# Degree sums of a graph network's adjacency build: added by GpSimd, or by transfers that add as they write

## The reference, cut to what matters

```
def _L0_gnn_ref(x, W_lin, W_agg, edge_index):
    row, col = (edge_index[0], edge_index[1])
    msgs = x[row]
    summed = jax.ops.segment_sum(msgs, col, num_segments=num_nodes)
    count = jax.ops.segment_sum(jnp.ones((row.shape[0],), x.dtype), col, num_segments=num_nodes)[:, None]
    agg = summed / jnp.maximum(count, 1.0)
    out = agg @ W_agg.T + x @ W_lin.T
    ...
```

## Time and profile before

| | |
|---|---|
| median of 3 runs | 3345.48 us (3345.35 to 3350.49) |
| span of the profiled execution | 3347.6 us |
| TensorE busy, of the span | 65% |
| VectorE busy | 68% |
| ScalarE busy | 25% |
| GpSimd busy | 49% |
| GpSimd's 48 additions (L633) | 159.9 us in all |
| build, first to last matmul | 360.4 to 848.3 us |

### The profile page before, as it was taken

The page is one execution under the profiler, slowest core; times in us unless marked ns, Lnnn a source line. Parts: engine busy times, 40 slices in busy tenths (PEclk is TensorE's granted clock), DMA queues, the critical chain, the costliest instruction groups (busy, mean ns, idle before and its releaser), DMA issues.

```text
span 3347.6 us, 46752 instructions
## 1 busy us (share of the span) xinstructions
PE 2186.4 (65%) x12603; PEld 1297.7 (39%) x12659; DVE 2262.1 (68%) x3125; ACT 846.9 (25%) x1397; POOL 1645.1 (49%) x1455
## 2 busy tenths in 40 slices
PE   0488877777895989995963444444567665528563
PEld 0233455454453455553443111111366621107563
DVE  8999898898558720055133454444987799979777
ACT  0099433232002020022100111111244322206442
POOL 7400133333047777777104777777876777710000
PEclk9799999999997999997986555565559999965897
DMA  2000010110443523400724433345348733530453
GB/s 71 0 0 0 25 49 39 44 44 39 148 137 84 164 60 96 94 1 1 158 59 94 117 113 112 112 116 104 93 153 268 240 110 110 107 37 0 134 175 94
DMA packets 195115, 301.52 MB, mean 90 GB/s; under 512 B 120540, under 2 KB 133818, under 8 KB 194922
## 3 DMA queue, kind: packets, MB, share of 16 engines
q1 hardware_dynamic: 138986, 175.88, 16.5%
q0 software_dynamic: 40512, 62.87, 10.3%
q10 hardware_dynamic: 15552, 61.94, 6.0%
HBM read 191.65 MB, written 88.01 MB: 84 GB/s over the span
## 4 chain that ended last, share of the span: by engine, by line
PE 35%; POOL 19%; issue 16%; DVE 16%; DMA 6%; ACT 5%; ACTq 1%; DVEq 0%; SPq 0%; POOLq 0%; PEldq 0%
POOL arena L1313 18%; PE PS L538 11%; PE PS L699 9%; PE PS L884 6%; DMA arena<-T_att,idx 5%; ACT arena L514 4%; DVE arena L559 4%; PE PS L981 3%; PE PS L476 2%; DVE arena L1204 1%; PE PS L968 1%; DVE arena L374 1%; DVE arena L490 1%; POOL W L1322 1%; DVE arena L567 1%
## 5 line engine op out<-in xcount | busy, mean ns | idle before, releaser
L1313 POOL DMA_INDIRECT arena<-T_att,idx x864 | 843.7, 976 | 316.9 <-issue 224.8
L538 PE MATMUL PS<-arena 128*128 128x400 f16 (+2 forms) x4320 | 782.5, 332 | 270.0 <-issue 109.7
L538 PEld LDWEIGHTS PS<-arena 128*128 128x128 f16 (+2 forms) x4320 | 529.9, 158 | 512.9 <-issue 349.8
L1148 DVE TENSOR_REDUCE arena<-PS 128x1024 f32 (+1 forms) x432 | 502.2, 1212 | 321.6 <-PE PS L1115 321.6
L1486 POOL DMA_INDIRECT order<-arena x400 | 504.8, 1262 | 246.5 <-issue 246.5
L559 DVE TENSOR_SCALAR arena<-arena 128x1600 f16<-128x1600 f16 x448 | 385.7, 905 | 64.4 <-PE PS L538 60.4
L1115 PE MATMUL PS<-arena,pick 128*128 128x512 bf16 x812 | 315.8, 488 | 157.0 <-DVE arena L1148 143.2
L699 PE MATMUL PS<-arena 128*128 128x512 f16 (+1 forms) x1575 | 317.6, 361 | 88.3 <-issue 75.2
L633 POOL TENSOR_TENSOR rdeg<-rdeg,arena 128x1600 f32<-128x1600 f32 x48 | 159.9, 3331 | 313.4 <-ACT arena L617 313.4
L1104 PE MATMUL PS<-ident_b,score_buf 128*32 128x128 bf16 x864 | 90.0, 268 | 307.1 <-ACT score_buf L1077 297.4
L699 PEld LDWEIGHTS PS<-arena 128*128 128x128 bf16 x1575 | 147.8, 99 | 254.1 <-issue 102.3
(11 more groups left out here) (257 smaller groups left out, 2786.0 us busy)
## 6 DMA issues: line engine op xcount, KB each, us to landing
spill<-arena SPq DMA_DIRECT2D x108, 560.0 KB, 2.8
arena<-spill ACTq DMA_DIRECT2D x108, 560.0 KB, 3.9
arena<-A SPq DMA_DIRECT2D x50, 800.0 KB, 4.5
A<-arena SPq DMA_DIRECT2D x50, 400.0 KB, 2.4
arena<-A SPq DMA_DIRECT2D x50, 400.0 KB, 3.2
arena<-T_att,idx POOLq DMA_INDIRECT x864
order<-arena POOLq DMA_INDIRECT x400
T_att<-h SPq DMA_DIRECT2D x2, 1600.0 KB, 12.3
```

What stands on the lines that cost most here:

```text
L538: return t.matmul(where, lhsT, rhs, start=False, stop=True, skip_group_check=True)
L1148: v.tensor_reduce(cmax[d][:, u:u + 2, bass.ds(i * SLOTS + half * GROUP + q // 2 * QUAD, QUAD)], PS[:, u * BANK:(u + 2) * BANK].rearrange(" ...
L1313: p.indirect_dma_start(out=ring1[:, b, j, :], out_offset=None, in_=T_att[d][:, :], in_offset=bass.IndirectOffsetOnAxis(ap=idx[:, d, k:k + ...
```

## The change

GpSimd no longer adds the strips. It clears `dst_sum` once, and for every cell, when ScalarE has written the strip, it issues a transfer from the strip (f16) to its half of `dst_sum` (f32) that adds to what is there. Two transfers to the same half must not overlap, so GpSimd waits for the one 2 cells before to land. Completion is counted in four semaphores, one for each strip buffer, where one semaphore counted the additions; all waits follow that.

```
-        cell_counted, dst_summed, dst_read = sem("cell_counted"), sem("dst_summed"), sem("dst_read")
+        dst_summed, dst_read = sem("dst_summed"), sem("dst_read")
+        cell_added = [sem(f"cell_added{s}") for s in range(RING_A)]
...
-                    a.wait_ge(cell_counted, c - RING_A + 1)
+                    a.wait_ge(cell_added[c % RING_A], 16 * (c // RING_A))
...
             p.wait_ge(lo_ready, 1)
+            pool_link(p.memset(dst_sum, 0.0))
             for c in range(CELLS):
                 at = dst_sum[:, c % BANDS * BW:(c % BANDS + 1) * BW]
                 p.wait_ge(cell_out, c + 1)
-                if c < BANDS:
-                    p.tensor_copy(at, stage[c % RING_A]).then_inc(cell_counted, 1)
-                else:
-                    p.wait_ge(cell_counted, c - BANDS + 1)
-                    p.tensor_tensor(at, at, stage[c % RING_A], ALU.add).then_inc(cell_counted, 1)
+                if c >= BANDS:
+                    before = c - BANDS
+                    p.wait_ge(cell_added[before % RING_A], 16 * (before // RING_A + 1))
+                p.dma_start(out=at, in_=stage[c % RING_A], accum_op=ALU.add).then_inc(cell_added[c % RING_A], 16)
+
+        def all_added(eng):
+            for s in range(RING_A):
+                eng.wait_ge(cell_added[s], 16 * len(range(s, CELLS, RING_A)))
...
-                t.wait_ge(cell_counted, CELLS)
+                all_added(t)
...
-            v.wait_ge(cell_counted, CELLS)
+            all_added(v)
             place_dve(v, 0)
...
-            a.wait_ge(cell_counted, CELLS)
+            all_added(a)
             ht_act(a, 0)
```

## The result

The changed kernel took 3319.88 us, the median of 4 runs (3318.59 to 3320.83), beside 3347.31 us for the kernel before (3345.35 to 3350.49): a ratio of 0.9918 [0.9904, 0.9932]. It is 27 us faster where 58 were forecast. The profiled spans, 3347.6 and 3319.0 us, differ by 28.6. The time lies in the range that the prediction gave, 3276 to 3336, but more than half of the forecast gain is missing, so a term of the sum was wrong.

A forecast was written before the change was run, and what follows sets the result against it. In the build, GpSimd's additions were taken to hold up VectorE's one-hots, so TensorE ran out of them. -63 + 3 + 2 = -58 us on the profiled 3347.6 made 3289.6, 3287.5 us as median; range 3276 to 3336.

The forecast's parts named there:

- the build: Build of A, 487.9 us long: removing GpSimd's additions was to save 63 us.
- from last strip to first product: End of the build: the last adding transfer was to delay the first strip's load of A by 2 us, ends 0 and 5.
- the prediction's floor and small waits: Build of A: 421.5 us from undisturbed matmul groups and the pauses between them, plus 3 us kept for small waits.
- L: Build: time from one adding transfer's start of issue to the next issue on the same half; 9 us, free below 16.
- the slow rival: Build: GpSimd's wait for landing transfers becomes the new bound, slower from 19.8 us per transfer, 3400 us at 22; chance 12%.
- The rival in which the port is still taken: Build: GpSimd's issues hold VectorE for their length, +22 us, 3310 us; chance 14% together with the clock rival.
- the memset: Before the build: clearing the sums was to hold up VectorE and add 3 us, bounds 0 and 3.3.
- That is the loading of the group's cell numbers (the longer one has the loop's branch besides), and the change leaves it.: Build: TensorE's stands between groups of 8 chunks, 0.89 and 1.31 us alternately, 60.3 us in all, stay as they are.
- so I take the clock at 1.00: Build: TensorE's granted clock rises from 0.94 to 1.00, so 18.9 us of matmul time goes.
- a transfer of over 14 us: Build: one of two signs that the forecast is wrong, one adding transfer taking over 14 us.
- The clock rival: Build: TensorE's clock stays as it is, +19 us, 3306 us; chance 14% together with the rival of the port still taken.
- the idle rival: Build: nothing comes of it, TensorE's stands only move to another wait inside the group, 3345 +- 6 us; chance 4%.

The follow-up runs named there:

- e1_noadd: The changed kernel with no strip added at all, the degree sums left at a constant: 3291.77 us, ratio 0.9836 to the kernel before.
- e12_again: The changed kernel run a second time with no edit: 3318.75 us, ratio 0.991 to the kernel before.
- e8_best: The changed kernel with f16 sums, transfers issued after the next group's first chunk, and plain first transfers instead of the memset: 3290.75 us, ratio 0.9826 to before.
- e11_high: The changed kernel with only the sums of partitions 64 to 127 added, the others constant: 3313.0 us, ratio 0.9897 to the kernel before.
- e10_low: The changed kernel with only the sums of partitions 0 to 63 added, the others constant: 3318.2 us, ratio 0.9913 to the kernel before.

## Why the prediction was right and wrong

**The sum, term by term**, from the two profiles: the build -41.4 us (forecast -63), its start +3.7 (+3), from last strip to first product 15.6 us instead of 13.1, +2.5 (+2), and behind that +6.7 (0). Together -28.5.

**Right: what bounded the build.** GpSimd's additions held up VectorE's one-hots, TensorE ran out of them, and both went away: the maximum of the one-hots is 0.67 us (under 1.3 forecast), their sum 275 (280), and the stands that are left are those between groups. e1_noadd gave 425.7 us for the build where the prediction's floor and small waits make 424.5.

**Right: the transfers as GpSimd and ScalarE see them.** L was 5.3 us with the issue in it, against an assumed 9 and a limit of 16, so no one waited for a landing and the slow rival never came near. Of the DMA engines a transfer took 3.1 us (3). The issue takes 0.86 us, at most 1.29, beside one-hots of 0.62: the Trainium skill, "SBUF — State Buffer", section "Who interferes with whom", says that descriptors written by GpSimd starve while VectorE is in a two-port mode; in this stage the longest issue is 0.4 us over the shortest. The rival in which the port is still taken is refuted: no one-hot is over 0.67 us.

**Right: the memset.** It took 2.76 us and the build began 3.7 later (2.6 in e12_again, the same kernel); with the memset gone, in e8_best, it begins at 360.39, as before.

**Wrong: the step "That is the loading of the group's cell numbers (the longer one has the loop's branch besides), and the change leaves it."** The prediction named the very instruction, counted it at 28 x 0.89 + 27 x 1.31 = 60.3 us, and took it as fixed, though it reads SBUF. TensorE's stands came to 76.3 - 60.3 = 16.0 us more, of which 2.0 are there without any addition (e1_noadd) and 14.0 are the loads'; the loads themselves grew by 55.2 - 36.0 = 19.2 us, some of it under matmuls still running. With it fell the next step, **"so I take the clock at 1.00"**: the reason given was "no longer stand than 1.3 us", stands became up to 2.49, the clock 0.96, and the matmuls took 370.8 - 361.2 = 9.6 us more. 16.0 + 9.6 = 25.6 us is the build's whole distance from its floor (446.5 - 421.5 = 25.0, with 0.6 us of stands before the first matmul), 3 of which were allowed for. Neither sign by which the forecast was to be known wrong came, a transfer of over 14 us (5.3) or a first product over 5 us later (2.5): both watched the transfers, none the loads. So the time is inside the stated range partly by luck: the range was made wide for the port, the clock and a long landing, and the lengthened loads were in no rival.

The prediction asked of the DMA engines' new work only whom it delays among the transfers (+2 us at the end of the build), and of the wider part, 0.37 more of all sixteen engines through 446 us, nothing. The row that it had to weigh was in the trace of before: the load's median of 593 ns and maximum of 1233. There, too, 12 of the 56 loads ran beside the store of a strip, with a mean of 939 ns, and the others had a mean of 596. A spread from 0.59 to 1.23 was the sign that the load depends on something. Bounded by it, 56 loads at most 0.64 us longer, the term would have been 0 to +36 us, and the step would have carried a doubt. The same section of "SBUF — State Buffer" in the Trainium skill says that transfers never contend with a compute engine and that TensorE never waits. For matmuls and one-hots the traces agree (6.47 us a group beside a full DMA, 0.67 us a one-hot). The load of registers by TensorE's sequencer, which the section doesn't mention, does wait: 599 ns without and 1321 with traffic, and the measurement decides.

**What the rivals got.** The clock rival had the right loss in part (+9.6 of its 19 us), by another way than it said. The port, the slow and the idle rival got nothing.

**What stays open**: what the load and the transfers share (not only a port of the load's own partition, by e11_high); why the lower half of the partitions costs 7 us more than the upper; how much of the 6.7 us behind the build belongs to the change; and whether a build with fewer registers per group, or an unrolled one, would do without the loads' stands of 60 us. The last was not tried.

## What to carry to other kernels

When a change gives the DMA engines more to do, ask of every instruction that reads memory on the way, also those of an engine's sequencer (register loads in loops above all), how it fares beside traffic; its minimum, median and maximum in the trace of before tell whether it cares. A stand of TensorE can cost twice when it grows: once by itself, and once by the clock behind it. Where transfers can't be avoided, make them short and give them a moment: here the same additions cost 21 us of the build issued as soon as possible, 10 issued behind the next group's load, and 1 so issued in half the bytes.

## What the runs showed of the hardware

- TensorE's register load from SBUF takes 0.59 us for 8 registers and 1.10 for 16, undisturbed; beside transfers up to 1.8 (2.7 in e10_low) and 3.3 us. The stores of the strips lengthen it too: in the kernel before to 0.94 us on average, 1.23 at most.
- A transfer that adds 128x1600 f16 to f32 in SBUF: issue by GpSimd 0.86 us, landing in 5.3, 3.1 us of all sixteen engines. Adding f16 to f16: 4.3 us and 2.2. On 64 partitions alone: 5.4 us, no less than on 128. On all 128 the engines' time goes roughly by the bytes read: 1.0 us for a store of 400 KB, 1.9 for the plain 800 KB, 2.2 for the f16 addition's 800, 3.1 for the 1200 of the change.
- TensorE's clock: in the changed kernel's build the granted clock stayed at 1.00 in the 39 groups behind stands of up to 1.74 us; in 9 of the 14 behind stands of 1.81 to 2.49 us it was at 0.50 for a part of the group (0.77 over the group), which made the group of 32 matmuls 0.8 to 1.0 us longer. The last stand alone doesn't decide it: in the kernel before, with stands inside groups as well, two groups behind stands of 0.90 and 0.93 us had 0.79 and 0.77.
- VectorE's 128x1600 one-hots, 0.62 us undisturbed, took at most 0.67 beside GpSimd's issues.
